# Channel neighbours of a stencil: from GpSimd and VectorE sums to accumulating transfers

## The chip, the cores and the metric

The kernel runs on one core of a Trainium2 chip. The metric is the device time of one execution in microseconds. All arithmetic is in float32 (weights of the gated stage are split into a high and a low part of float32r). The engines are called by their short names: PE (TensorE, matmul), DVE (VectorE), ACT (ScalarE), POOL (GpSimd) and SP (SyncE, which here only issues transfers).

## The reference, cut to what matters

Four residual stages follow each other on x of 2 x 2048 x 512 (batch, time, channel). x1 comes from a masked attention pooling. The second stage is a reaction-diffusion step on each batch's 2048 x 512 plane; it is what the change touches:

```python
    def _L1_cond_ref(y, zX, zY, zR, dx, dy):
        yp_x = jnp.pad(y, ((0, 0), (0, 0), (1, 1)), mode='reflect')
        lap_x = (yp_x[:, :, :-2] - 2.0 * y + yp_x[:, :, 2:]) / (dx * dx)
        yp_y = jnp.pad(y, ((0, 0), (1, 1), (0, 0)), mode='reflect')
        lap_y = (yp_y[:, :-2, :] - 2.0 * y + yp_y[:, 2:, :]) / (dy * dy)
        du_dt = zX[:, :, None] * lap_x + zY[:, :, None] * lap_y + zR[:, :, None] * y * (1.0 - y)
        return du_dt
...
    x = x + _L0_cond_ref(x, L0_cond_W1, L0_cond_b1, L0_cond_v, itok_B_0_2)
    x = x + _L1_cond_ref(x, condB_zX[:, None], condB_zY[:, None], condB_zR[:, None], 1, 1)
    x = x + _L2_cond_ref(x, itok_B_0_6, L2_cond_down_w, L2_cond_down_b, L2_cond_up_w, L2_cond_up_b, L2_cond_ln_g, L2_cond_ln_b)
    x = x + _L3_cond_ref(x, L3_cond_tau_ctx, condB_tauraws, ...)
```

So x2 at channel e is a term in x1 at e, a term in its square, the two neighbours in time times zY, and the two neighbours in channel, e-1 and e+1, times zX; at the edges the one neighbour counts twice. The third stage is an adapter (down, relu, up) with layer norm, the fourth a gated recurrence with several 512 x 512 matmuls.

## The kernel before, in words

Time is cut into 32 tiles of 128 rows (16 per batch), and four tiles make a group: 8 groups, counted (batch, j) in the first part and 0 to 7 in the second. Every engine has its order of work written out by hand, with semaphores between engines.

The **first part** (up to about 190 us) makes x1 and x2 for all 32 tiles. A `tile(b, c)` on PE is the pooling matmuls of tile c (`pooled`, L990 and L991) and the time part of the stencil of the tile eight before it (`time_part`, L1001 and L1003: the diagonal and time neighbours as a matrix of 128 x 128, and the rows across tile edges, which SP brings by the small transfers of `edges`). On DVE a tile is `x1` (L1375) and `mix` (L1389), which adds -zR times the square, made by ACT in `squares` (L661) in the group's slot of sqb, to the time part from PSUM. There are two slots in sqb (j % 2), each of one group.

The channel neighbours: POOL's `channel_part` (L541 to L544) adds x1 shifted by one channel either way into one slot, xr[:, 1], with two slivers for the edges. DVE's `stencil` (L1398) adds zX times this sum to the group's slot of sqb, and raises x2_done. SP then stores the group (`store_x2`, L374) to DRAM, except group 0, which goes straight to xr[:, 0]. The next squares of that slot waits for the store, the next channel_part for the stencil.

Group 0 goes on into the adapter within the first part: PE turns it (`x2_transposes`, L1037), ACT evicts that (`x2_evict`, L676), PE multiplies (`down`, L1047), ACT applies relu (L680), PE multiplies again (`up`, L1063 and L1064). Meanwhile `add_rows` on POOL (L550) adds a bias row from DRAM to xr[:, 0] by an accumulating transfer. DVE's `y_sum` (L1454) adds both and waits for that transfer. `ln_moments` on ACT, `rstd` on POOL, `ln_weigh` (L1461) and `ln_apply` (L1467) on DVE are the layer norm; then `x3_transposes`, `x3_evict` on ACT and `x3_lo` on DVE prepare the second part.

The **second part** is a loop over the 8 groups: `front(g)` (first 12 matmuls against wn1, then wg), soma, temporal and output, all of three matmuls for each product; within group g the adapter of group g+1 runs, whose x2 SP loads from DRAM (`load_group`, L98) into xr[:, (g+1) % 2].

Each engine's queue is in order: a wait holds back all that stands behind it. SP's queue holds the loads, edges and stores in the order of its block. What ties squares to the stores is:

```python
                        if n == 2:
                            act.wait_ge(x2_done, 1)
                        elif n > 2:
                            act.wait_ge(x2_out[j % 2], 16 * ((n - 2 + j % 2) // 2))
                        act.activation(sqb[:, j % 2], xb[:, b, part(j)], ACT.Square).then_inc(sq_act, 1)
```

## Time and profile before

| | us |
|---|---|
| median of 3 runs | 756.19 (756.01 to 758.79) |
| the profiled execution's own time | 756.09 |
| its span, first to last instruction | 754.3 |
| PE busy | 711.4 |
| DVE busy | 554.5 |
| ACT busy | 337.4 |
| POOL busy | 117.5 |

The span leaves out 1.8 us of the execution's own time. All rows below come from this one execution. In them "x8" is a count, busy time is in us and a mean in ns; what stands in square brackets or behind the last bar is the idle time of the engine just before, and what ended it. PEld is PE's weight load, which overlaps its matmuls; PEclk is the clock that PE was granted as a share of the full 2.4 GHz. A line number is that of the kernel before. A DMA share of 1 means that the core's 16 DMA engines were all busy.

### The profile page before, as it was taken

How to read it: one execution, taken by the hardware profiler on the slowest of the kernel's cores; microseconds unless marked ns; L12 is line 12 of the kernel's file. 1: busy time of each engine (PE TensorE's matmuls, PEld its weight loads, DVE VectorE, ACT ScalarE, POOL GpSimd, SP SyncE). 2: the span in 40 equal slices, each digit the busy share in tenths (PEclk: the TensorE clock that was granted, in tenths of full speed). 3: DMA queues.
4: the chain of work that ended last, by engine and by line, in shares of the span. 5: the costliest groups of instructions: out<-in, count | busy, mean ns of one | idle time of the engine just before them, and what ended most of it. 6: DMA issues, size and time to landing. Idle time of an engine off the chain costs nothing.

```text
span 754.3 us, 8249 instructions
## 1 busy us (share of the span) xinstructions
PE 711.4 (94%) x2936; PEld 514.9 (68%) x2936; DVE 554.5 (74%) x787; ACT 337.4 (45%) x706; POOL 117.5 (16%) x195
## 2 busy tenths in 40 slices
PE   4998986977899999999999999999999999999986
PEld 1554443534686877787787868786877788687864
DVE  3686894699798669758875986597668758875954
ACT  2244424323445724563465257344724553464144
POOL 5002032244002100210021021002100210111001
PEclk9999998998999999999999999999999999999999
DMA  7993036312620033011303020330033011301001
GB/s 218 373 343 116 15 103 158 120 58 85 221 45 13 1 111 56 1 56 56 56 0 113 12 45 1 112 52 5 1 111 57 0 56 57 56 1 57 0 1 56
DMA packets 35295, 56.55 MB, mean 75 GB/s; under 512 B 6380, under 2 KB 8428, under 8 KB 35254
## 3 DMA queue, kind: packets, MB, share of 16 engines
q1 hardware_dynamic: 27542, 47.62, 18.2%
q0 software_dynamic: 4224, 8.39, 7.1%
q10 hardware_dynamic: 3488, 0.01, 0.3%
q8 instruction: 23, 0.38, 0.2%
q14 instruction: 18, 0.15, 0.1%
HBM read 40.16 MB, written 15.73 MB: 74 GB/s over the span
## 4 chain that ended last, share of the span: by engine, by line
PE 81%; DVE 9%; issue 3%; ACT 3%; DMA 2%; SPq 1%; POOLq 0%; DVEq 0%; POOL 0%; ACTq 0%
PE bank L1007 19%; PE bank L1009 19%; PE bank L1008 19%; PE bank L1047 4%; PE bank L1064 4%; PE bank L903 3%; PE bank L1111 2%; PE bank L1071 2%; PE bank L1001 2%; PE bank L990 2%; PE bank L1037 2%; DVE sqb L1389 1%; DMA x_scratch<-sqb 1%; DMA sqb<-in_xT 1%; DVE sqb L1398 1%
## 5 line engine op out<-in xcount | busy, mean ns | idle before, releaser
L1007 PE MATMUL bank<-xh,wg_l 128*128 128x512 f32 x256 | 104.1, 407 | 0.1
L1009 PE MATMUL bank<-xh,wg_h 128*128 128x512 f32 x256 | 100.2, 391 | 0.0
L1008 PE MATMUL bank<-xl,wg_h 128*128 128x512 f32 x256 | 99.8, 390 | 0.0
L1504 DVE TENSOR_TENSOR_SCAN tr<-alpha,carry,tr 128x512 f32<-128x512 f32 x48 | 58.9, 1268 | 0.0
L1007 PEld LDWEIGHTS bank<-xh,wg_l 128*128 128x128 f32 x256 | 48.3, 189 | 12.5 <-issue 2.7
L1008 PEld LDWEIGHTS bank<-xl,wg_h 128*128 128x128 f32 x256 | 48.1, 188 | 12.1 <-issue 2.0
L1009 PEld LDWEIGHTS bank<-xh,wg_h 128*128 128x128 f32 x256 | 48.1, 188 | 11.0
L1007 PE MATMUL bank<-th,wt_l 128*128 128x512 f32 x128 | 53.5, 418 | 2.0 <-DVE tl L1516 2.0
L1007 PE MATMUL bank<-xh,ws_l 128*128 128x512 f32 x128 | 53.4, 417 | 0.0
L1007 PE MATMUL bank<-wo_h,pl 128*128 128x512 f32 x128 | 50.6, 395 | 0.8 <-DVE pl L1526 0.8
L1483 DVE TENSOR_TENSOR_SCAN hb<-alpha,carry,bank 128x512 f32<-128x512 f32 x24 | 30.5, 1271 | 28.2 <-PE bank L1009 28.2
L1008 PE MATMUL bank<-tl,wt_h 128*128 128x512 f32 x128 | 50.6, 395 | 0.0
L1009 PE MATMUL bank<-th,wt_h 128*128 128x512 f32 x128 | 50.4, 394 | 0.0
L1009 PE MATMUL bank<-xh,ws_h 128*128 128x512 f32 x128 | 49.9, 390 | 0.0
L1008 PE MATMUL bank<-wo_l,ph 128*128 128x512 f32 x128 | 49.9, 390 | 0.0
L1009 PE MATMUL bank<-wo_h,ph 128*128 128x512 f32 x128 | 49.8, 389 | 0.0
L1008 PE MATMUL bank<-xl,ws_h 128*128 128x512 f32 x128 | 49.8, 389 | 0.0
L541 POOL TENSOR_TENSOR xr<-xb 128x2040 f32<-128x2040 f32 x8 | 28.8, 3600 | 133.1 <-DVE sqb L1398 57.0
L1498 DVE SCALAR_TENSOR_TENSOR tr<-wgb,blend_w,mod 128x512 f32<-128x512 f32 x64 | 45.3, 749 | 3.6 <-ACT mod L714 2.8
L1522 DVE SCALAR_TENSOR_TENSOR wide<-wide,soma 128x512 f32<-128x512 f32 x32 | 22.1, 689 | 31.7 <-ACT wide L744 31.7
L728 ACT ACTIVATE carry<-tr 128x2 f32<-128x2 f32 x32 | 6.5, 203 | 85.2 <-DVE tr L1504 85.2
L744 ACT ACTIVATE wide<-bank,bias_temp 128x512 f32<-128x512 f32 x32 | 22.1, 690 | 46.5 <-PE bank L1009 46.5
(220 smaller groups left out, 1593.3 us busy)
## 6 DMA issues: line engine op xcount, KB each, us to landing
xb<-in_x SPq DMA_DIRECT2D x8, 1024.0 KB, 14.5
xr<-rows_scratch POOLq DMA_DIRECT2D x8, 1024.0 KB, 9.6
x_scratch<-sqb SPq DMA_DIRECT2D x7, 1024.0 KB, 4.4
xr<-x_scratch SPq DMA_DIRECT2D x7, 1024.0 KB, 5.6
result<-xr SPq DMA_DIRECT2D x7, 1024.0 KB, 4.3
xb<-in_xT SPq DMA_DIRECT2D x3, 1024.0 KB, 10.9
xt<-in_xT SPq DMA_DIRECT2D x2, 1024.0 KB, 6.6
sqb<-in_xT SPq DMA_DIRECT2D x2, 1024.0 KB, 10.3
```

Source lines behind the costliest of these rows:

```text
L541: po.tensor_tensor(q[:, :, 1:E - 1], xg[:, :, 0:E - 2], xg[:, :, 2:E], ALU.add)\
L744: act.activation(wide[:, k], bank[TEMP[k]][:], ACT.Tanh, bias=bias_temp[:, k:k + 1], scale=0.5).then_inc(gate_act, 1)
L903: last = pe.matmul(bank[HID[b][j]][:], w1_sb[:, k], xt_slot[b][j][:, k], start=(k == 0), stop=(k == KE - 1))
L1007: pe.matmul(acc, wl, xh_, start=start, stop=False)
L1008: pe.matmul(acc, wh, xl_, start=False, stop=False)
L1009: return pe.matmul(acc, wh, xh_, start=False, stop=stop)
L1047: last = pe.matmul(bank[DOWN][:], dw[:, b, k], x2t(q)[:, k], start=(k == 0), stop=(k == KE - 1))
L1064: pe.matmul(bank[UP(q)[c]][:], z[:, chunk(c)], uw[:, b], start=False, stop=True)\
L1483: ve.tensor_tensor_scan(h, alpha[:, 0:1].broadcast_to([P, GN]), bank[CTX[k]][:], 0.0 if first else carry[:, k, 0:1], ALU.mult, ALU.add)\
L1498: ve.scalar_tensor_tensor(t[:, d], w, blend_w[:, d, k:k + 1], mod[:, d], ALU.mult, ALU.mult).then_inc(tr_in, 1)
L1504: ve.tensor_tensor_scan(t[:, d], alpha[:, 1 + d:2 + d].broadcast_to([P, GN]), t[:, d], 0.0 if first else carry[:, k, 1 + d:2 + d], ALU.mul ...
L1522: ve.scalar_tensor_tensor(wide[:, k], wide[:, k], 1.0, soma[:, k], ALU.add, ALU.mult).then_inc(prod, 1)
```

## The change

The channel neighbours are no longer summed on chip. ACT makes a copy of each group of x1 times zX (`scaled`), 514 wide, with the reflected channel at either edge. It lies where xr[:, 1] was, and 8 elements beyond. SP stores it to a new DRAM tensor (`store_xz`). DVE's mix is now the last step before x2 is stored; the stencil is gone, and with it channel_part. POOL then issues for each group two accumulating transfers (`add_neighbours`): the copy read from its column 0, and, once that has landed, from its column 2, each 512 wide, added in DRAM to x2 (for group 0, in SBUF to xr[:, 0]). load_group waits for these additions.

```diff
+                    def add_neighbours(q):
+
+                        dst = xr[:, 0] if q == 0 else x2_g[:, q:q + 1].rearrange("p u c e -> p (u c) e")
+                        src = xz_g[:, q:q + 1].rearrange("p u c e -> p (u c) e")
+                        po.wait_ge(xz_out, 16 * (q + 1))
+                        if q == 0:
+                            po.wait_ge(mixed, GT)
                         else:
-                            po.wait_ge(x2_done, k)
...
+                            po.wait_ge(x2_out[q % 2], 16 * ((q + 1) // 2))
+                        for i in (0, 2):
+                            if q or i:
+                                po.wait_ge(xz_add, 16 * (2 * q + i // 2))
+                            po.dma_start(dst, src[:, :, i:i + E], accum_op=ALU.add).then_inc(xz_add, 16)
...
-                    for j in range(NG):
-                        channel_part(0, j)
+                    add_neighbours(0)
+                    add_neighbours(1)
                     po.wait_ge(rows_out, 16 * B)
                     add_rows(0)
-                    channel_part(1, 0)
-                    channel_part(1, 1)
                     for c in range(GT):
                         rstd(ln_ss, ss_a, EPSILON, rs_a, c, ln_p, ln_rs, c)
-                    channel_part(1, 2)
-                    channel_part(1, 3)
+                    add_neighbours(2)
...
+                        if g + 3 < GROUPS:
+                            add_neighbours(g + 3)
...
+                    def scaled(b, j):
+                        n, xg, zx_b = NG * b + j, xb[:, b, part(j)], coef[:, ZX, b:b + 1]
+                        act.wait_ge(x1_done, NT * b + GT * (j + 1))
+                        if n:
+                            act.wait_ge(xz_out, 16 * n)
+                        else:
+                            act.wait_ge(masks_set, S_MASKS)
+                        act.activation(xz[:, :, 1:E + 1], xg, ACT.Copy, scale=zx_b).then_inc(xz_set, 1)
+                        act.activation(xz[:, :, 0:1], xg[:, :, 1:2], ACT.Copy, scale=zx_b).then_inc(xz_set, 1)
+                        act.activation(xz[:, :, E + 1:E + 2], xg[:, :, E - 2:E - 1], ACT.Copy, scale=zx_b)\
+                           .then_inc(xz_set, 1)
...
+                    def store_xz(b, j):
+                        u = NG * b + j
+                        sp.wait_ge(xz_set, 3 * (u + 1))
+                        sp.dma_start(xz_g[:, u:u + 1].rearrange("p u c e -> p (u c) e"), xz).then_inc(xz_out, 16)
+
                     def store_x2(b, j):
                         u = NG * b + j
-                        sp.wait_ge(x2_done, u + 1)
+                        sp.wait_ge(mixed, GT * (u + 1))
...
                     edges(0, 3)
+                    store_xz(0, 3)
                     store_x2(0, 1)
...
                     edges(1, 2)
+                    store_xz(1, 2)
                     store_x2(1, 0)
                     edges(1, 3)
+                    store_xz(1, 3)
                     store_x2(1, 1)
```

On SP each store_xz stands right behind its group's edges, ahead of the stores of x2 that stood there. On ACT's queue the squares move behind the scaled copies and edge_high, and from the first evictions on to other places. Three places show it. First, ACT from the squaring of group (0, 2) on to the eviction of the transposed x2 (`prob<-bank`); `probT<-bank` is probT_evict, `edge_hl` edge_high. Before:

```order
L661 ACTIVATE sqb<-xb 128x2048
L636 ACTIVATE g_hl<-bank 128x512
L642 ACTIVATE bw_hl<-bank 64x512 x2
L668 ACTIVATE edge_hl<-edge,coef 64x512
L642 ACTIVATE bw_hl<-bank 64x512 x2
L651 ACTIVATE probT<-bank 128x512 x2
L661 ACTIVATE sqb<-xb 128x2048
L651 ACTIVATE probT<-bank 128x512 x2
L668 ACTIVATE edge_hl<-edge,coef 64x512
L661 ACTIVATE sqb<-xb 128x2048
L676 ACTIVATE prob<-bank 128x512 x4
```

Now, from the same squaring on (`xr_all<-xb,coef` is scaled; xr and xz are now views of xr_all):

```order
L692 ACTIVATE sqb<-xb 128x2048
L670 ACTIVATE probT<-bank 128x512 x4
L680 ACTIVATE xr_all<-xb,coef 128x4x512
L681 ACTIVATE xr_all<-xb,coef 128x4
L682 ACTIVATE xr_all<-xb,coef 128x4
L699 ACTIVATE edge_hl<-edge,coef 64x512
L692 ACTIVATE sqb<-xb 128x2048
L680 ACTIVATE xr_all<-xb,coef 128x4x512
L681 ACTIVATE xr_all<-xb,coef 128x4
L682 ACTIVATE xr_all<-xb,coef 128x4
L707 ACTIVATE prob<-bank 128x512 x4
```

The squaring of (0, 2) stood ahead of the block evictions (`bw_hl`) and stands behind them now, right ahead of the probT evictions; that of (0, 3) stood between these and follows scaled(0,3) now.

Second, ACT at the layer norm of group 0 (`hb,ss_a` are its moments). Before, squares(1,1) and its edge row stand ahead of the first moments:

```order
L661 ACTIVATE sqb<-xb 128x2048
L668 ACTIVATE edge_hl<-edge,coef 64x512
L686 ACTIVATE nmu_a<-sum_a 128x1
L689 ACTIVATE hb,ss_a<-tr,nmu_a 128x512
L686 ACTIVATE nmu_a<-sum_a 128x1
```

Now, from the last moments on:

```order
L717 ACTIVATE nmu_a<-sum_a 128x1
L720 ACTIVATE hb,ss_a<-tr,nmu_a 128x512
L692 ACTIVATE sqb<-xb 128x2048
L680 ACTIVATE xr_all<-xb,coef 128x4x512
L681 ACTIVATE xr_all<-xb,coef 128x4
L682 ACTIVATE xr_all<-xb,coef 128x4
L699 ACTIVATE edge_hl<-edge,coef 64x512
L692 ACTIVATE sqb<-xb 128x2048
```

squares(1,1) follows all four moments now, and scaled(1,2) lies between it and squares(1,2).

Third, POOL around the row add of group 0. Before, with two groups' sums on either side:

```order
L541 TENSOR_TENSOR xr<-xb 128x4x510
L543 TENSOR_SCALAR xr<-xb 128x4
L544 TENSOR_SCALAR xr<-xb 128x4
L550 DMA xr<-rows_scratch 128x4x512
L541 TENSOR_TENSOR xr<-xb 128x4x510
```

Now:

```order
L559 DMA xr_all<-xz_scratch 128x4x512 x2
L559 DMA x_scratch<-xz_scratch 128x4x512 x2
L564 DMA xr_all<-rows_scratch 128x4x512
L570 TENSOR_TENSOR rs_a<-ss_a,consts 128x1
L572 TENSOR_TENSOR rs_a<-rs_a,consts 128x1
```

The row add stood behind sums on POOL itself; it stands behind four accumulating transfers, of which each but the first waits for the one ahead to land.

Elsewhere: on PE, x2_transposes(0), down(0) and up(0) come two, two and one tiles later; on DVE y_sum(0, 0) comes one tile later and ln_weigh and ln_apply are spread among the tiles. weight_hi waits for the last mix instead of the last stencil. At the start, v, b1, ptype, zx, zy, zr and the profile ids are loaded from ACT's queue, ahead of its ten parameters, not from SP's, so that SP goes straight on with the loads of x transposed; tanh and v's copy wait for v and b1 alone, and PE runs twelve warm-up matmuls on a tile of ones:

```diff
+                    pe.wait_ge(ones_set, 1)
+                    for i in range(WARM):
+                        pe.matmul(bank[REP[0]][:, 0:P], ones[:], ones[:], start=True, stop=True)
+                    pe.wait_ge(w1_in, 16)
                     hidden(0, 0)
                     hidden(0, 1)
+                    pe.wait_ge(v_set, 1)
                     scores(0, 0)
```

## Rows read from the trace of the kernel before

**Rows 1.** The page's head: busy time of each engine

```profile
PE 711.4 (94%) x2936; PEld 514.9 (68%) x2936; DVE 554.5 (74%) x787; ACT 337.4 (45%) x706; POOL 117.5 (16%) x195
```

**Rows 2.** Busy time of each engine by stage: PE, PEld, DVE, ACT, POOL, granted clock, DMA

```profile
100.00:151.40 51.40, 42.50 (x129) 22.34 (x127) 34.77 (x50) 15.94 (x26) 13.32 (x10) 0.90 0.45 126
151.40:188.50 37.10, 27.40 (x76) 14.11 (x74) 35.80 (x36) 11.17 (x17) 18.02 (x17) 0.86 0.20 72
...
201.00:754.00 553.00, 544.51 (x2370) 427.39 (x2368) 406.04 (x555) 266.00 (x590) 66.87 (x127) 1.00 0.16 41
```

**Rows 3.** The chain that ended last, 100 to 135 us: start, us, what

```profile
108.25 5.38 DMA x_scratch<-sqb
...
115.53 1.06 ACT probT L651 x2
...
120.39 4.32 DMA x_scratch<-sqb
...
126.61 1.56 ACT prob L676 x3
...
128.31 5.36 PE bank L1047 x8
```

**Rows 4.** Groups on ACT, 0 to 200 us: busy, mean ns, idle before

```profile
L661 ACT ACTIVATE sqb<-xb 128x2048 f32<-128x2048 f32 x8 | 15.3, 1909 | 57.2 <-DMA x_scratch<-sqb 37.6 <-DVE xb L1375 13.6 <-DVE xr L1398 6.0
```

**Rows 5.** Groups on DVE, 100 to 200 us, same columns

```profile
L1398 DVE SCALAR_TENSOR_TENSOR sqb<-xr,coef,sqb 128x2048 f32<-128x2048 f32 x7 | 16.5, 2352 | 0.3
...
L1467 DVE SCALAR_TENSOR_TENSOR xr<-tr,rs_a,xr 128x512 f32<-128x512 f32 x4 | 5.7, 1464 | 0.0
```

**Rows 6.** Instructions by time, start and us: the last block eviction on ACT, then PE

```profile
99.41 0.59 ACT L642 ACTIVATE bw_hl<-bank 64x512 fp32r<-64x512 f32 x1 [1.17 <-PE bank L991]
...
103.88 1.53 PE L990 MATMUL bank<-xb,probT 128*128 128x512 f32 x2 [2.60 <-DVE g_hl L1370]
...
107.76 1.05 PE L990 MATMUL bank<-xb,probT 128*128 128x512 f32 x2
...
109.97 1.03 PE L972 MATMUL bank<-ident,prob 128*128 128x128 f32 x8
```

**Rows 7.** DMA queues of the page: packets, MB, share of 16 engines' span

```profile
q1 hardware_dynamic: 27542, 47.62, 18.2%
q0 software_dynamic: 4224, 8.39, 7.1%
```

**Rows 8.** Stretches with one accumulating transfer, and with one plain store

```profile
128.00:130.00 2.00, 1.69 (x2) 0.84 (x3) 0.00 (x0) 1.24 (x3) 0.00 (x0) 0.50 1.12 182
266.00:268.00 2.00, 2.00 (x10) 1.64 (x9) 0.00 (x0) 0.00 (x0) 0.00 (x0) 1.00 1.03 383
```

**Rows 9.** DMA issues: count, KB, median us from issue to landing

```profile
xr<-rows_scratch POOLq DMA_DIRECT2D x8, 1024.0 KB, 9.6
x_scratch<-sqb SPq DMA_DIRECT2D x7, 1024.0 KB, 4.4
...
xt<-in_wsoma SPq DMA_DIRECT2D x1, 1024.0 KB, 8.1
```

**Rows 10.** Two instants by time, the last y_sum(0) on DVE, then PE

```profile
150.67 0.69 DVE L1454 SCALAR_TENSOR_TENSOR tr<-bank,xr 128x512 f32<-128x512 f32 x1
...
188.28 0.39 PE L1009 MATMUL bank<-xh,wn_h 128*128 128x512 f32 x1
...
196.87 3.51 PE L1111 MATMUL bank<-nar,wn_rep 128*128 128x512 f32 x4 [2.36 <-ACT nar L704]
```

**Rows 11.** The start by time, all engines

```profile
2.34 0.43 SPq L381 DMA_DIRECT2D v_sb<-in_v  x1
...
5.84 3.14 ACTq L581 DMA_DIRECT2D bias_temp<-in_btemp  x1
...
10.65 1.28 ACT L646 ACT_TABLE_LOAD   x1 [10.65 <-issue]
...
18.95 1.02 PE L916 MATMUL bank<-hid,v_rep 128*128 128x512 f32 x2
```

More of the change, by code:

```diff
@@ L799, in _ @@
                     wg_hi(0, wg_h[:, 0:KE], xt0[:])
-                    squares(0, 0)
+                    scaled(0, 0)
                     weights(1, 1)
@@ L803, in _ @@
                     edge_high(0, 0)
+                    squares(0, 0)
                     weights(1, 2)
                     wg_hi(1, wg_h[:, KE:], xr[:, 0])
-                    squares(0, 1)
                     weights(1, 3)
+                    scaled(0, 1)
                     block_exps(1)
@@ L810, in _ @@
                     prob_exps(1)
+                    squares(0, 1)
                     wg_hi(2, wn1_h[:], xt0[:, :, 0:A])
                     sums_raw(1)
-                    squares(0, 2)
+                    scaled(0, 2)
                     sums_hi(1)
@@ L833, in _ @@
                     act.activation(ln_g_row[:], ln_g_row[:], ACT.Copy, scale=SQRT_E).then_inc(rows2_set, 1)
-                    squares(1, 1)
+                    scaled(1, 1)
                     edge_high(1, 1)
```

128 lines of the change are left out of this document (59 added, 69 removed).

## The prediction

> **What bounds the kernel now.** I read first the busy share of each engine, then the stages, then the chain that ended last, then the groups behind its waits. The page shows TensorE (PE) busy 94% of 754.3 us [rows 1]. By stage [rows 2], PE is busy 544.5 of 553.0 us from 201 us on, at full clock: the loop over the eight groups is PE's own work, and the change puts no instruction of PE, DVE or ACT into it. All that can be won or lost lies before 201 us. From 100 to 151.4 us PE is busy 42.5 of 51.4 us, from there to 188.5 only 27.4 of 37.1 us, with DVE busy 35.8. The chain between 100 and 135 us shows what PE waits for [rows 3]: a store of x2 (5.4, then 4.3 us), for which ACT's next squaring waits, and behind it on ACT's queue the evictions (probT at 115.5, the transposed x2 at 126.6) that PE needs for the adapter at 128.3. ACT stood idle 57.2 us ahead of its eight squarings [rows 4]. So two things bound the stretch: DVE's work, and stores with ACT's queue behind them.
>
> **What DVE gets back.** Eight stencils leave DVE, 2.35 us each (seven in the group shown, the eighth writes xr): 18.8 us [rows 5]. POOL's eight neighbour sums leave too. Beside them ln_apply cost 1.46 us on average; a stencil runs at 0.59 us for 512 columns, 0.7 with an instruction's own start, so its four would give back 3 us more [rows 5]. I take 22 us off DVE, nearly all of it between 90 and 189 us. ACT gets eight scaled copies of 128x2048, each 1.91 us as for a squaring [rows 4], with two slivers of about 0.2: 2.25 us each, 18 us in a queue that had 57 us of idle time ahead of squarings. Both are off the end-setting path only as long as nothing else on ACT or in the DMA queues is late; that is what fails, I think.
>
> **What is added to the DMA engines.** Eight stores of the copy at 1.05 MB and sixteen accumulating transfers of 1.05 MB. The nearest row is the rows' accumulating transfer [rows 9]: 9.6 us from issue to landing. Its queue holds eight, 8.39 MB, 7.1% of 754.3 us: 0.071 x 754.3 / 8 = 6.7 us of all 16 engines each, so 2.9 us lie around it. The plain queue costs 0.182 x 754.3 / 47.62 = 2.9 us for a million bytes, 3.0 for a transfer [rows 7]. While one add runs, the engines are busy 1.12 at 182 GB/s; a plain transfer gives 383 GB/s at 1.03 [rows 8]. An add thus fills the engines by itself. Ten of the sixteen are issued inside the loop, where 69 us per group (553 / 8) hide them. Six adds (groups 0 to 2) and add_rows(0) share 90 to 185 us with plain transfers.
>
> **Stage one, to the last y_sum of group 0** (151.4 us now [rows 10]). ACT runs much as now up to its last block eviction, which ends at 100.0 [rows 6]; then squares(0,2) (1.9) stands ahead of the first probT eviction (0.5), so PE's tile(1,0) starts at 102.5, where now it waits for DVE until 103.9. The next tile takes 2.2 us, 107.76 to 109.97, and the one behind the wait 3.9 at the lower clock; after a wait half as long I take 5.2 for both: 107.7. Eight transposes (0.9), the evictions (0.6) and scaled(0,3) (2.25) end at 111.5. SP then issues store_xz(0,3) and, at 112.1, store_x2(0,1). The second of two such transfers lands 7.0 (4.4 + 3.0 less 0.4) to 8.1 us after its issue [rows 9]: 119.7. Here POOL's order matters. Its queue is in order and each add waits for the one ahead: add one of group 1 is issued at 119.7 and lands 9.6 later, the second is issued, and add_rows(0) right behind it on the same queue, so 2.9 + 2 x 6.7 = 16.3 more: the row add lands at 145.6 at the earliest. In that time SP's queue carries about four plain transfers (the rest of x2(0,2), xz(1,0), x2(0,3), xz(1,1), with wtemp behind them): 4 x 3.0 = 12 us, of which 2.9 fit into the gap between the adds. Shared in turn that is 9.1 us more: 154.7. PE's up(0), a tile later in its order, would be done near 140.5 (squares(0,3) can end only at 121.6, behind the 119.7; then some nineteen microseconds of PE's work), and DVE would stand ready near 143.4; so y_sum(0,0) waits for the row add. Two y_sum, a tile, edge_low, two y_sum: 4.7 us. The end of the stage: 150.3 without sharing, 159.4 with it, against 151.4. By row 8, where one add alone fills the engines, I take 159.4: **+8.0**; the other end is **-1.1**.
>
> The Trainium skill ("DMA: Bandwidth & Descriptors", Anatomy of one DMA) fits a transfer issued by GpSimd with 2.0 us and the bytes over 436 GB/s. The 9.6 us row disagrees: by the rule a megabyte would land in 4.4 us, and this stage would end at 148.1.
>
> **Stage two, to the end of the first 12 matmuls of front(0)** (188.7 us now, so 37.3 after stage one [rows 10]). ACT's order: ln_moments(0,3) 1.4 us, squares(1,1) to +3.3 (DVE's mix(1,4) waits 2.3 us for it), scaled(1,2) to +5.6, then SP issues xz(1,2) and x2(1,0) at +6.0. squares(1,2) waits for the latter: landed at +13.0, squared by +14.9, scaled(1,3) to +17.2, xz(1,3) and x2(1,1) land at +24.6, squares(1,3) ends +26.5. Behind it on ACT stands x3_evict(0), on DVE mix(1,12), mix(1,13) and x3_lo(0): four pairs of evictions at 1.15 us, the last subtraction and three matmuls, 6.1 us, so +32.6. The two adds of group 2 run beside it (POOL issues them after the four rstd, at +2.4 and about +14): the first shares with the first pair of stores, 5.2 us, the second with the tail of the next, 0.5. So +38.3, **+1.0** against now; without sharing +32.6, **-4.7**.
>
> **Stage three, to PE's return to full work.** Now the matmuls for mod start at 196.9 and take 3.5 us at the lower clock, 11.7 us after stage two's end [rows 10]. Afterwards mix(1,15) ends 0.7 us after it; two weight_hi, the table load and the gelu (1.8, 1.8, 1.3, 0.7) give 6.3, and the matmuls 1.8 at full clock: 8.1 or so, **-3.6**. The wait for the last stencil goes.
>
> **The start, 0.** SP drops seven small issues (0.43 us for one [rows 11]) and its big loads begin 4 us sooner, but the same seven go ahead of ACT's others. ACT's table load stands behind its last issue at 10.65, then bw_zeros (2.2 us), then tanh(0,0); one of its issues took 3.14 us in the time of SP's loads. Seven at 0.5 put the load at 14.1, tanh(0,0) ends at 18.3 to 18.9, and PE's first score matmul, at 18.95 now, stays where it is. If ACT's issues stall behind loads that start sooner, +3. The warm-up matmuls stand in PE's idle time.
>
> **Sum**: 8.0 + 1.0 - 3.6 + 0 = +5.4 on the profiled execution's own 756.1 us, which equals the median of 756.2: **761.5 us**. By the terms' own bounds (start, landings a microsecond either way) 758.5 to 767.
>
> **Rivals.**
> Rival A, faster: adds and plain transfers overlap on the engines, since an add may wait on memory more than it moves. Then -1.1 - 4.7 - 3.6 = -9.4: 746.7 us. For it: 22 us off DVE, and the busy share is the packets' time, which can hide idle time. Against it: row 8's 1.12. The skill's "Arbitration" paragraph (same page) has each engine serve its queues in turn, packet by packet; no row here shows two of them at work, and by it the forecast's sum would hold.
> Rival B, no change: half the sharing, (5.4 - 9.4) / 2 = -2.0: 754 us.
> Rival C, the adds into x2 in DRAM are dearer than the row's into SBUF, say 9 us of engine time: the two adds of group 1 bring stage one 4.6 more, 766 us. It decides once they take longer than 8 us.
>
> **Chances.** Forecast 0.42, A 0.32, B 0.20, C 0.06. 0.5% (3.8 us) is about what a measurement of this kernel can tell from no change. Faster 0.33, same 0.23, slower 0.44. Range 746.5 to 767: it reaches A's time, as its 0.32 cannot be left out, and C's.
>
> **What would show it.** Right: y_sum(0,0) waits for the row add's landing past 150 us; squares(0,3), (1,2), (1,3) wait for x2 stores that land over 9 us after issue; the six early adds land 10 to 15 us after issue; from then on 69 us per group as now. Wrong: stores landing in 5 to 8 us beside an add; y_sum(0,0) waiting for PE; PE's scores before 17 us or after 21; an add that lands in under 7 us; a loop group longer than now, which would mean the late adds hold back load_group.

## The result, and the profile after

The change makes the kernel slower: 770.07 us (median of four runs, 769.68 to 772.44) against 756.1, a ratio of 1.0205 with a 95% interval from 1.0177 to 1.0232. The forecast was 761.5 us with a range from 746.5 to 767: the sign was right, the size was not, and the time lies outside the range. The kernel before, run again beside the experiments, had medians from 754.2 to 756.0 and single runs from 751.3 to 758.4, so differences of two medians below about 2 us are not read here.

| profiled execution | before | after |
|---|---|---|
| own time / span, us | 756.09 / 754.3 | 769.78 / 768.0 |
| PE's second batch of score matmuls begins | 24.14 | 34.57 |
| end of stage one (last y_sum of group 0) | 151.36 | 165.20 |
| end of stage two (first 12 matmuls of front(0)) | 188.67 | 204.61 |
| end of the first mod matmuls | 200.38 | 211.92 |
| one group of the loop | 70.48 | 71.01 |

The page of the kernel after, the busy times (against [rows 1]), the DMA queues (packets, MB, share of 16 engines' span; against [rows 7]) and the DMA issues (count, KB each, median us to landing; against [rows 9]):

```profile
PE 720.4 (94%) x2960; PEld 521.7 (68%) x2960; DVE 527.8 (69%) x779; ACT 356.4 (46%) x730; POOL 102.0 (13%) x187
...
q1 hardware_dynamic: 30900, 56.04, 21.3%
q0 software_dynamic: 12672, 25.17, 20.1%
q10 hardware_dynamic: 4354, 0.02, 0.4%
...
x_scratch<-xz_scratch POOLq DMA_DIRECT2D x14, 1024.0 KB, 11.0
xz_scratch<-xr_all SPq DMA_DIRECT2D x8, 1028.0 KB, 7.6
...
xr_all<-rows_scratch POOLq DMA_DIRECT2D x8, 1024.0 KB, 9.8
x_scratch<-sqb SPq DMA_DIRECT2D x7, 1024.0 KB, 7.6
```

DVE lost 26.7 us of work and POOL 15.5, and PE is busy for the same share of the span as before. The change did what it says; the time went elsewhere. The same split into stages as in [rows 2], of the kernel after (length, then busy time of PE, PEld, DVE, ACT, POOL, granted clock, DMA share, GB/s):

```profile
110.43:165.20 54.77, 43.06 (x123) 23.55 (x124) 23.64 (x41) 21.66 (x34) 7.12 (x8) 0.89 0.97 249
165.20:204.61 39.41, 27.68 (x71) 14.53 (x70) 20.82 (x33) 18.17 (x25) 3.97 (x6) 0.76 0.65 165
211.92:766.00 554.08, 547.57 (x2373) 426.89 (x2371) 406.82 (x556) 267.46 (x590) 78.50 (x137) 1.00 0.29 63
```

In stage one the DMA engines are now busy 0.97 of the time where it was 0.45. DVE is busy 23.6 us of 54.8 (before: 34.8 of 51.4). Stage two has PE at 27.7 of 39.4 us. The loop (last row) is PE's own work as before, 547.6 of 554.1 us.

The start, instructions by time (start and duration in us; in square brackets the idle time before and what ended it), against [rows 11]:

```profile
8.57 3.57 ACTq L594 DMA_DIRECT2D bias_g<-in_bg  x1
12.18 2.49 ACTq L594 DMA_DIRECT2D bias_soma<-in_bsoma  x1
14.70 2.88 ACTq L594 DMA_DIRECT2D bias_temp<-in_btemp  x1
17.60 3.22 ACTq L594 DMA_DIRECT2D bias_n<-in_bn  x1
20.85 1.28 ACT L665 ACT_TABLE_LOAD   x1 [20.85 <-issue]
...
25.18 2.05 PE L955 MATMUL bank<-hid,v_rep 128*128 128x512 f32 x2 [9.46 <-ACT hid L621]
```

Four issues of ACT take 2.5 to 3.6 us each, the table load stands behind them and comes at 20.85 instead of 10.65 us, and PE waits 9.46 us for the first tanh. PE's second batch of score matmuls begins 10.4 us later than before. Then the waits the forecast spoke of, on POOL, DVE and ACT:

```profile
128.11 1.28 POOL L559 DMA_DIRECT2D x_scratch<-xz_scratch  x1 [15.69 <-DMA x_scratch<-sqb]
141.38 1.25 POOL L559 DMA_DIRECT2D x_scratch<-xz_scratch  x1 [11.99 <-DMA x_scratch<-xz_scratch]
142.13 1.83 POOL L564 DMA_DIRECT2D xr_all<-rows_scratch  x1
...
160.46 0.69 DVE L1488 SCALAR_TENSOR_TENSOR tr<-bank,xr_all 128x512 f32<-128x512 f32 x1 [6.86 <-DMA xr_all<-rows_scratch]
...
127.68 1.91 ACT L692 ACTIVATE sqb<-xb 128x2048 f32<-128x2048 f32 x1 [7.51 <-DMA x_scratch<-sqb]
...
183.87 1.91 ACT L692 ACTIVATE sqb<-xb 128x2048 f32<-128x2048 f32 x1 [12.57 <-DMA x_scratch<-sqb]
...
195.24 1.91 ACT L692 ACTIVATE sqb<-xb 128x2048 f32<-128x2048 f32 x1 [6.57 <-DMA x_scratch<-sqb]
```

The x2 store lands 7.5 us after ACT is ready for squares(0,3). POOL issues the two adds of group 1 at 128.1 and 141.4, and the row add 0.8 us behind the second; it lands 18 us later (DVE goes on at 160.46, having waited 6.86). squares(1,2) waits 12.57 us, squares(1,3) 6.57.

Last, the first matmul of two groups of the loop, in the kernel after:

```profile
272.66 0.39 PE L1046 MATMUL bank<-xh,wn_l 128*128 128x512 f32 x1
...
343.67 0.39 PE L1046 MATMUL bank<-xh,wn_l 128*128 128x512 f32 x1
```

and in the kernel before, the same two groups:

```profile
260.76 0.39 PE L1007 MATMUL bank<-xh,wn_l 128*128 128x512 f32 x1
...
331.24 0.39 PE L1007 MATMUL bank<-xh,wn_l 128*128 128x512 f32 x1
```

71.01 us for a group against 70.48. PE's busy share hides it, since PE is busy nearly all the time in both.

The difference of the spans, 13.7 us, is then: start +10.4, stage one +3.4 (130.6 against 127.2 us from the second score matmuls), stage two +2.1, stage three -4.4, the rest +2.2. The rest is the loop up to its last group, nearly seven groups at +0.53 or 3.6 us, less a last group 1.4 us shorter. The span behind the last group's first matmul is either near 69.2 or near 70.8 us in the traces of all kernels of this study, whatever the change. For that, and for when the first loads land, the experiments are read by their stages first.

### The profile page after: what moved, and what is told of

Read it like the earlier page. It is cut to its first block, busy times and chain, and to the rows that moved or that the text cites. A ratio compares the mean times of both kernels' runs of the same rounds, so it can differ in the third digit from the quotient of the medians.

```text
span 768.0 us, 8320 instructions
## 1 busy us (share of the span) xinstructions
PE 720.4 (94%) x2960; PEld 521.7 (68%) x2960; DVE 527.8 (69%) x779; ACT 356.4 (46%) x730; POOL 102.0 (13%) x187
## 3 DMA queue, kind: packets, MB, share of 16 engines
q10 hardware_dynamic: 4354, 0.02, 0.4%
## 4 chain that ended last, share of the span: by engine, by line
PE 79%; DMA 6%; DVE 6%; issue 3%; ACT 3%; ACTq 3%; POOL 0%; SPq 0%; POOLq 0%; DVEq 0%
PE bank L1048 19%; PE bank L1046 19%; PE bank L1047 19%; DMA x_scratch<-sqb 4%; PE bank L1103 3%; PE bank L1086 3%; PE bank L942 3%; DMA xr_all<-rows_scratch 2%; ACTq L594 2%; PE bank L1150 2%; PE bank L1029 2%; PE bank L1076 2%; PE bank L1110 2%; PE bank L1040 1%; PE bank L955 1%
## 5 line engine op out<-in xcount | busy, mean ns | idle before, releaser
L1047 PEld LDWEIGHTS bank<-xl,wg_h 128*128 128x128 f32 x256 | 48.1, 188 | 13.7 <-issue 1.9
L1040 PE MATMUL bank<-xb,uw 128*128 128x512 f32 x64 | 38.8, 692 | 13.4 <-DVE sqb L1432 13.4
```

The lines of the kernel that those rows point to most:

```text
L1040: pe.matmul(acc, time_m[:, b], xb[:, b, c], start=True, stop=False)
L1047: pe.matmul(acc, wh, xl_, start=False, stop=False)
```

## The experiments

Two theories to begin with. S, for the start: ACT's issues stall. D, for stages one and two: an add fills the DMA engines, so that plain stores and the row add beside it are late. Rivals: R1, the start's delay is absorbed later; R3, ACT's longer queue and the order of the stores. The code cuts of this part are shortened: a line names what moved, not the code word for word. "The kernel with the start undone" is s1_start_back, and a stage one is counted from PE's second score matmuls.

### s1_start_back: the start undone

```diff
 sp: w1; load_xt(0, 0)
+sp: b1, v, ptype, zx, zy, zr, profile
 sp: load_xt(0, 1..3); load_x(0, 0..3)
...
-act: v, b1, ptype, zx, zy, zr, profile
 act: the ten parameter loads
```

> The changed kernel, with the seven small loads (b1, v, ptype, zx, zy, zr, profile) back on SP between load_xt(0, 0) and load_xt(0, 1), as before; the warm-up matmuls and all of the stencil's change stay. Theory S: the seven loads on ACT push ACT's issues into the time of SP's big loads, where one takes 2.5 to 3.6 us, so the table load comes at 20.85 us where it came at 10.65, and all behind it is 10.4 us late. It expects tanh(0,0) back at 14.5 us, PE's first scores at 19 us and 770.1 - 10.4 = 759.7 us. Rival R1, the start's delay is mostly taken up later by waits that are there anyway (the row add, the stores of x2): 764 us or more.

Measured: 764.3 us (763.1 to 767.1). Table load at 11.46, second scores at 26.11 us: 8.5 us of the 10.4 came back there, 5.7 of the medians, 6.7 of the two profiled executions. S's 759.7 is missed by 4.6 us, and the median lies at the edge of what R1 gave (764 or more). But R1's reason, that later waits take the delay up, is not what the trace shows. Of the 3.7 us missing between the profiled executions, 2.0 us is this execution's own start (PE waited 3.7 us for xT's second part), 1.6 us is stage one (132.2 us from the second scores, after: 130.6). Its remainder against the kernel before, without the start's 2.0, is +5.0 in stage one, +2.3 in stage two, -4.4 in stage three and +2.1 behind it.

### s2_start_alone: only the start, in the kernel before

```diff
-sp: seven small loads between load_xt(0, 0) and load_xt(0, 1)
+act: the same seven ahead of the ten parameter loads
+pe: twelve warm-up matmuls ahead of hidden(0, 0)
```

> The kernel before, with the change of the start alone (seven small loads on ACT ahead of its ten, SP's big loads sooner, twelve warm-up matmuls); the stencil as before. Theory S: 756.1 + 10.4 = 766.5 us. Rival R1: 756 to 762 us, since in this kernel too stores and POOL would take up a part.

Measured: 764.1 us (761.9 to 766.2), ratio 1.011 (1.006 to 1.016). The profiled execution has 766.23, 10.1 more than before, with second scores at 34.44 and stage one at 161.1: the delay goes through whole. The median has it at 8.0, between R1's 762 at most and S's 766.5. R1 falls, and S's size is an upper end: the start costs 8 to 10 us in this kernel too, which has the old stencil.

### s3_params_on_sp: the ten parameter loads on SP

```diff
-act: ten parameter loads behind the seven
+sp: the ten, behind load_x(0, 3)
```

> The changed kernel, with ACT's ten parameter loads moved to SP behind the last load_x(0, 3), the seven small ones staying on ACT. It tells the count of issues on ACT from the order of the seven. Theory S (what hurts is ACT issuing at all after SP's big loads began to queue): ACT's seven end at 4.5 us, the table load comes there, tanh(0,0) follows PE's hidden(0,0) at about 11.4 us instead of 24.35, and PE is steady some 2 us sooner than before: 770.1 - 12 = 758 us, 755 to 761. Rival R2 (the first scores wait for the small loads' data, not for ACT's issues, since their packets queue behind SP's): tanh(0,0) not before 18 us, 764 us or more.

Measured: 769.5 us, no gain where I expected 755 to 761. The first half of theory S held: table load at 4.70, first scores at 15.59 instead of 25.18. But the same loads now stall SP. SP's issues and PE's next wait:

```profile
14.82 4.63 SPq L396 DMA_DIRECT2D taus<-in_tau_ctx  x1
...
38.49 0.50 SPq L350 DMA_DIRECT2D xt<-in_xT  x1
...
43.75 4.73 PE L942 MATMUL bank<-xt,w_sb 128*128 128x512 f32 x6 [10.05 <-DMA xt<-in_xT]
```

SP spends 14.8 to 30 us on them, load_xt(1, 0) goes out at 38.49 where it went at 28.16, and PE waits 10.05 us for it. R2 got its time (764 or more) but not its reason, as the first scores came before 18 us. The stall thus belongs to these loads in this stretch, not to ACT.

### s12_x_late: x behind hidden(0, 0)

```diff
 sp: load_xt(0, 0..3)
+sp: wait hid_mm >= 1
 sp: load_x(0, 0..3)
```

> The changed kernel with one wait more: SP issues the four loads of x (4 MB) only when PE has ended hidden(0,0), near 11 us, instead of at 3.9 us. All seventeen small loads stay on ACT in the same order. Theory S1 (ACT's issues stall since SP's large loads are queued in the DMA engines in that time, not since there are seventeen of them): ACT's last issue ends near 10 us instead of 20.8, tanh(0,0) comes at 14 to 15 us, PE's scores at 16 to 19, the whole 9 to 11 us less than the change: 759 to 761 us. Rival S2 (small loads on ACT's queue get slow behind one another after the first ten, whatever SP does): the last issue still ends after 17 us and the time stays over 766 us.

Measured: 770.1 us, no change:

```profile
11.41 3.31 SPq L354 DMA_DIRECT2D xb<-in_x  x4
...
20.65 1.28 ACT L666 ACT_TABLE_LOAD   x1 [20.65 <-issue]
```

The loads of x go 7.5 us later, ACT's table load still comes at 20.65. Theory S1 as I had put it, that the loads of x are the cause, falls. Rival S2 got its numbers, and it was the next run that told it from the right one. In 12 to 21 us the trace of the kernel after has these two queues (q1 is SP's, q10 ACT's small loads; packets, MB, share):

```profile
q1 hardware_dynamic: 1605, 3.19, 98.2%
q10 hardware_dynamic: 1604, 0.01, 11.7%
```

1605 packets of about 2 KB and 1604 of a few bytes: one for one. In the kernel before, in 6 to 12 us, SP's queue had little behind its seven small issues and moved 0.77 MB. In those 6 us the two queues show:

```profile
q1 hardware_dynamic: 1254, 0.77, 40.6%
q10 hardware_dynamic: 2471, 0.01, 22.9%
```

2471 small packets in 6 us, 412 a microsecond, against 178 a microsecond above. With x late, SP's queue had moved 2.7 MB by 12 us, less than the 4 MB of xT, so xT alone kept it filled until x followed. The Trainium skill ("DMA: Bandwidth & Descriptors", Queues, rings and completion order, its paragraph on arbitration) has each DMA engine go round the queues packet by packet; 1605 to 1604 agrees, in packets as the profile counts them.

### s14_gap: SP's queue kept dry until ACT's loads have landed

```diff
 sp: load_xt(0, 0)
+sp: wait params_in (all ten)
 sp: load_xt(0, 1..3); load_x(0, 0..3)
```

> The changed kernel, in which SP issues load_xt(0, 1) and all large loads behind it only when ACT's ten parameter loads have landed; the seventeen small loads stay on ACT in the same order. Between 12 and 21 us the changed kernel's traces show 1605 packets of SP's queue (2 KB each) and 1604 of ACT's (4 bytes mostly): one for one. In the kernel before, SP's queue ran nearly dry from 6 to 12 us, and ACT's moved 2471 packets in that time. Theory P (ACT's loads are thousands of packets of a few bytes, which queue packet for packet behind SP's large ones, and an issue waits for room in the queue): with SP's queue dry behind load_xt(0, 0), ACT's last issue ends near 11 us, all its packets are through by 13 us, and PE's scores, now behind load_xt(0, 1), begin near 20 us, so that PE is steady near 26 us instead of 34.6: 760 to 763 us. Rival S2 (ACT's issues stall by their own number): last issue after 17 us, 768 us or more.

Measured: 763.7 us (761.9 to 764.4), 6.4 less than the change, with all seventeen loads on ACT in the same order. ACT's last issue and table load, and the two queues in 6 to 12 us:

```profile
9.84 0.53 ACTq L596 DMA_DIRECT2D bias_n<-in_bn  x1
10.39 1.28 ACT L667 ACT_TABLE_LOAD   x1 [10.39 <-issue]
```

```profile
q10 hardware_dynamic: 4063, 0.02, 36.7%
q1 hardware_dynamic: 128, 0.23, 9.9%
```

No issue takes over 1.3 us, the last ends at 10.4, and 4063 small packets pass in 6 us, 677 a microsecond. Second scores at 27.52 (expected 26), and the time 0.7 us above P's 760 to 763. S2 falls: the number of issues on ACT was the same. What theory P says of the two queues holds; that a stalled issue waits for room in its queue is inferred, since a trace shows how long an issue takes and not what it waits for. The change closed the gap in SP's queue in which these 4354 packets used to get through (3488 of them on ACT before).

### s4_no_adds: the start undone, no adds

```diff
 add_neighbours(q):
-    two dma_start(dst, src, accum_op=add)
-pe, sp: waits on xz_add
+pe: wait mixed >= GT;  sp: wait x2_out[1] >= 16
```

> As the kernel with the start undone, and without the sixteen accumulating transfers of the neighbours: nothing is issued, and what waited for them waits for mix or for the stores of x2. The neighbours in channel are left out of x2. The scaled copies and their stores stay. Theory D (an add keeps all DMA engines busy for 6.4 us, so plain stores and the row add beside it are longer): the row add lands within 10.5 us of its issue and y_sum(0,0) waits for PE or DVE at about 143, stage one ends at 148, stores of x2(1,0) and x2(1,1) land in 7 us each; 12 to 13 us less than with the start undone: 747 us, 744 to 750. Rival R3 (ACT's longer queue, the scaled copies and the stores' waits without any sharing, is what offsets DVE's 22 us): within 4 us of the kernel with the start undone, 756 us or more.

Measured: 751.5 us (749.9 to 753.5), 12.8 less than with the adds. D's 12 to 13 less held; its 744 to 750 was counted from the 759.7 expected of the start undone, and is missed by 1.5. The form is the one that theory D gave: stage one 125.5 us from the second scores instead of 132.2, stage two 34.7 instead of 39.6, y_sum(0,0) without a wait. R3 falls. But half of what R3 names is still there. ACT's waits for stores of x2, with no add beside them:

```profile
120.23 1.91 ACT L688 ACTIVATE sqb<-xb 128x2048 f32<-128x2048 f32 x1 [7.69 <-DMA x_scratch<-sqb]
...
163.54 1.91 ACT L688 ACTIVATE sqb<-xb 128x2048 f32<-128x2048 f32 x1 [6.61 <-DMA x_scratch<-sqb]
...
174.88 1.91 ACT L688 ACTIVATE sqb<-xb 128x2048 f32<-128x2048 f32 x1 [6.54 <-DMA x_scratch<-sqb]
```

squares(0,3) waits 7.69 us as it did with the adds; squares(1,2) waits 6.61 instead of 12.3. So even without adds, and with 26.7 us of DVE's work gone, stage one is only 1.7 us shorter than in the kernel before (125.5 against 127.2) and stage two 2.6 us. And a group of the loop takes 71.01 us here too, so the loop's 0.53 us has nothing to do with the late adds.

### s9_plain_copies: copies instead of adds

```diff
-po.dma_start(dst, src[:, :, i:i + E], accum_op=ALU.add)
+po.dma_start(dst, src[:, :, i:i + E])
```

> The kernel with the start undone, in which the sixteen transfers of the neighbours are plain copies and not accumulating ones (same source, target, size, queue and waits; x2 becomes one shifted copy, which leaves out the rest of the second stage). The adds were 6.4 to 6.7 us of all engines each and 11.0 us from issue to landing. Theory M (it is the accumulation, not the transfer from DRAM to DRAM or the queue of POOL, that fills the engines): a copy takes 3 us of the engines and lands 5 to 6 us after its issue, and most of the 12.8 us between this kernel with and without adds is gained: 753 to 756 us. Rival M2 (a transfer from DRAM to DRAM costs as much without the addition): 762 us or more.

Measured: 752.7 us, 11.6 of the 12.8 us between the kernels with and without adds. POOL's queue and the transfers' landing (with the adds, in the kernel with the start undone: 20.0% of 761.2 us, and 11.4 us):

```profile
q0 software_dynamic: 8576, 25.17, 14.8%
...
x_scratch<-xz_scratch POOLq DMA_DIRECT2D x14, 1024.0 KB, 6.7
```

The eight row adds of the same queue cost 6.9% of 750.5 us in the kernel without the others, 51.8 us. That leaves 59.4 us for sixteen copies, 3.7 each, and (152.2 - 51.8) / 16 = 6.3 us for an add. M's numbers for a copy were low (3 us of the engines and 5 to 6 us to landing expected, 3.7 and 6.7 measured), but M holds in kind and M2 falls: of an add's 6.3 us, a copy the same way costs 3.7.

### s5_rows_first: the row add ahead of group 1's adds

```diff
 add_neighbours(0)
-add_neighbours(1)
 add_rows(0)
+add_neighbours(1)
```

> The kernel with the start undone, in which POOL issues the row add of group 0 (add_rows(0)) ahead of the two adds of group 1 instead of behind them. With the start undone alone, the row add was issued at 135.0 us, landed 18.4 us later, and y_sum(0,0) began at 153.5, some 6.5 us after DVE stood ready for it; the kernel's median was 764.3 us. Theory D (the row add is late since it shares the engines with group 1's second add and plain stores): now it is issued when PE has turned x2, near 129 to 131, lands in 10 to 13 us, y_sum(0,0) no longer waits for it, and begins at about 147: 5 to 6 us less, 757 to 760 us. Group 1's adds go later, to 130 to 165 us, where group 2's first store can meet them: if that costs, up to 3 us come back. Rival R4, the wait at y_sum is not what sets the end: 762 us or more.

Measured: 752.3 us (750.8 to 754.4), 12 less where I expected 5 to 7. POOL's issues, and y_sum(0,0):

```profile
127.31 1.28 POOL L571 DMA_DIRECT2D xr_all<-rows_scratch  x1 [22.77 <-PE bank L1077]
128.06 1.85 POOL L566 DMA_DIRECT2D x_scratch<-xz_scratch  x1
...
144.08 0.68 DVE L1489 SCALAR_TENSOR_TENSOR tr<-bank,xr_all 128x512 f32<-128x512 f32 x1
```

The row add is issued at 127.3, y_sum(0,0) waits for nothing, and stage one takes 122.4 us from the second scores, 9.8 less; stage two 36.7, 2.9 less. The wait was 6.5 us of that. Another 1.7 stood already at squares(0,3), ahead of anything that this run changes, and is scatter of the executions; some 1.6 us came between there and y_sum, where group 1's adds no longer run beside the stores. The last part is inferred, no run takes it by itself. R4 falls.

### s8_x2_first: stores of x2 ahead of the copies' stores

```diff
 edges(0, 3)
-store_xz(0, 3)
 store_x2(0, 1)
+store_xz(0, 3)
...
-store_xz(1, 2)
 store_x2(1, 0)
+store_xz(1, 2)
...
-store_xz(1, 3)
 store_x2(1, 1)
+store_xz(1, 3)
```

> The kernel with the start undone, in which SP issues store_x2 ahead of store_xz at the three places where both stand together (x2(0,1) ahead of xz(0,3), x2(1,0) ahead of xz(1,2), x2(1,1) ahead of xz(1,3)). With the start undone alone, squares(0,3), (1,2) and (1,3) waited 7.6, 12.3 and 6.8 us for those stores, each issued behind the scaled copy and its store. Theory Q (the order in the queue is half of what these waits cost: a store of x2 stands behind a scaled copy of 2.3 us and a store of 1.05 MB, 3 us of the engines): the three squares come 4 to 5 us earlier each; the last two waits are a chain that sets stage two's end, and the sum is 6 to 10 us: 755 to 758 us. Rival D2 (the adds' share of the engines alone makes the stores late, not the order): 761 us or more.

Measured: 749.5 us (747.7 to 751.3), 14.8 less where I expected 6 to 10; with the start undone and this alone it is faster than the kernel before, ratio 0.9925 (0.990 to 0.995). ACT's squares:

```profile
115.44 1.91 ACT L693 ACTIVATE sqb<-xb 128x2048 f32<-128x2048 f32 x1 [3.93 <-DMA x_scratch<-sqb]
...
162.09 1.91 ACT L693 ACTIVATE sqb<-xb 128x2048 f32<-128x2048 f32 x1 [1.04 <-DMA x_scratch<-sqb]
...
174.69 1.89 ACT L693 ACTIVATE sqb<-xb 128x2048 f32<-128x2048 f32 x1
```

The waits of 7.6, 12.3 and 6.8 us are 3.9, 1.0 and none. Stage two takes 28.0 us instead of 39.6. A scaled copy stood ahead of each store in two queues: the store waited for ACT's copy, and shared the engines with the copy's store. No run tells these two apart. Theory Q holds, and gives more than its 6 to 10 us; D2 falls: with the adds still there, the swap takes 11.6 us out of stage two, where taking the adds away took 4.9.

### s6_before_spread: the kernel before with a mended start

```diff
 (the change's start, in the kernel before)
-act: seven of the parameter loads ahead of the table load
+act: four of them behind tanh(0, 2), three behind tanh(0, 3)
```

> The kernel before with the changed start (seven small loads on ACT, SP's big loads sooner, warm-up matmuls), and eight of ACT's ten parameter loads mended: the first three stay where they are, four are issued behind tanh(0,2) and three behind tanh(0,3), when SP's first loads have landed. The stencil as before. With ten on SP the scores began at 15.6 us (before: 18.95) but SP's own next loads came 10 us late. Theory S: ACT's ten issues end near 6 us, PE's scores begin at 15.6 us, nothing is late behind, and the kernel is 3.3 us faster than before: 752 to 753.5 us against 756.1. Rival R5 (issues on ACT stall until 20 us wherever they stand, or the parameters come too late for block_exps): 756 us or more.

Seven loads moved in fact, four and three, where the expectation says eight. Measured: 757.4 us (753.2 to 760.3), no gain where I expected 3.3 us. The scores began at 15.03, 3.9 us sooner, and at the end of stage one nothing of it was left (151.35 against 151.36). PE waited 2.2 us for load_xt(1, 0) and 1.9 for ACT, which waited 6.6 us for the last parameter load. R5's time came (756 or more), by its second reason. In this kernel, what the start gains, the next loads take.

### s11_rows_x2: both orders changed

```diff
 (s5_rows_first and s8_x2_first together)
```

> The kernel with the start undone and both changes of order together: add_rows(0) ahead of group 1's adds on POOL, store_x2 ahead of store_xz on SP at the three places. Alone they measured 752.3 and 749.5 us, against 764.3. With store_x2 first alone, y_sum(0,0) still waited 8.7 us for the row add, and stage one ended at 154.9 us, stage two 27.7 us later. Theory D+Q (both wait chains are independent: the row add sets stage one, the stores set stage two): stage one ends at 147, stage two takes 28 to 31, the sum is 741 to 745 us, 11 to 15 less than before. Rival D3 (group 1's adds, pushed from 116 to 140 us into 128 to 155 us, make the stores of stage two late, as the gain of one is paid with the other): 747 to 752 us.

Measured: 739.3 us (737.0 to 744.1), ratio 0.980 (0.977 to 0.982). Stage one takes 119.3 us from the second scores, stage two 34.0; squares(1,2) and (1,3) wait again, 5.9 and 3.9 us, as group 1's adds are there now. So D3 is right in kind for this execution (stage two gives back 6 us of 11.6), while the median is 1.7 us under the 741 to 745 of D+Q.

What stage two gives back is not the same in every execution. These are POOL's second transfer of that stage and squares(1,3), first here and then in s18_pad128 (below), which has the same two orders:

```profile
155.06 1.28 POOL L566 DMA_DIRECT2D x_scratch<-xz_scratch  x1 [6.33 <-DMA x_scratch<-xz_scratch]
167.73 1.91 ACT L693 ACTIVATE sqb<-xb 128x2048 f32<-128x2048 f32 x1 [3.87 <-DMA x_scratch<-sqb]
```

```profile
159.99 1.28 POOL L567 DMA_DIRECT2D x_scratch<-xz_scratch  x1 [9.92 <-DMA xz_scratch<-xr_all]
163.67 1.90 ACT L694 ACTIVATE sqb<-xb 128x2048 f32<-128x2048 f32 x1
```

Here the add goes out at 155.06, ahead of the store of x2(1,1) at 157.51, and squares(1,3) waits 3.9 us for that store. There it goes out at 159.99, behind the store at 158.05, squares(1,3) doesn't wait, and stage two takes 27.9 us. The other traces with both orders have the add first and 33.7 to 35.3 us. The profiled execution of this kernel is also its slowest of six, 744.1. That the six runs' range of 7 us comes from these two outcomes fits, but is not shown.

### s13_rows_x2_late: the same with the change's own start

```diff
 (s11_rows_x2, with the start of the change, and s12_x_late)
```

> The changed kernel, its start kept, with all three: the loads of x behind hidden(0,0), the row add ahead of group 1's adds, x2's stores ahead of the copies'. Theory S1 and D+Q: as the kernel with the start undone and both orders changed, within 3 us, 740 to 746 us, since the small loads' place is then worth nothing either way. Rival S2: 750 us or more.

Measured: 752.0 us (746.8 to 754.0). Table load at 18.98, second scores at 32.80, 8.7 us later than in s11_rows_x2. S2's 750 or more is met. The expectation of "within 3 us" rested on the delay of x mending the start, and that s12_x_late had disproved. The difference, 12.6 us of the medians and 6.5 of the profiled executions, is the start's price once more, with the scatter of s11_rows_x2 in it.

### The loop: s17_before_shift and s15_pad

The first is the kernel before with 32 unused bytes of each partition behind xr, the second the kernel after with 32 more behind xr_all (64 in all).

```diff
 xr = sb("xr", [P, 2, GT, E])
+sb("shift", [P, 8])
```

> The kernel before, with nothing changed but 8 unused elements (32 bytes of each partition) declared behind xr. Theory L: a group of the loop takes 71.01 us instead of 70.48 and the kernel 756.1 + 4.2 = 760.3 us. Rival L2: 70.48 us and no change.

> The changed kernel, with 8 unused elements (32 bytes of each partition) declared behind xr_all, so that every tile behind it lies 64 bytes, not 32, further on than in the kernel before. In every kernel with the new stencil a group of the loop takes 71.01 us, also in the one without adds; in the kernel before and in the one with the start changed alone 70.48. The matmuls of wn and wg, 108 of a group, follow each other at 233.3 ns there and at 229.0 ns before. Theory L (it is the 32 bytes by which xr_all is longer than xr: tiles that PE reads lie at another offset): 70.48 us for a group again, 8 x 0.53 = 4.2 us less: 766 us. Rival L2 (the later adds and load_group, or the order of DVE and ACT around them, cost PE half a microsecond for each group): 71.01 us as now and 769 to 771 us.

Measured for the first: 758.5 us (755.7 to 761.7), ratio 1.0054 (1.003 to 1.0079), and for a group of the loop

```profile
261.10 0.39 PE L1008 MATMUL bank<-xh,wn_l 128*128 128x512 f32 x1
...
332.11 0.39 PE L1008 MATMUL bank<-xh,wn_l 128*128 128x512 f32 x1
```

71.01 us: the kernel before takes on the longer group by nothing but the shift. L2 falls. Its median is 3.5 us above that of the kernel before run beside it (754.96), and seven groups at +0.53 give 3.7. Measured for the second: 768.2 us, a group at 70.90 us, where I had expected 70.48 and 766 us. The place of the tiles decides, but 64 bytes don't restore it.

The traces also narrow down which matmuls are slower. Those of xh and xl against wg follow each other at 229.0 ns (median) in the kernel before and at 233.3 in the kernel after and in s17_before_shift. Those of ws, wt and wo stay at 227 in all three. By the order of declaration wg lies ahead of xr and is not moved, while xh and xl lie behind it and are; ws, wt and wo and what they are multiplied with lie all behind it and move together. So it is not the place of xh alone, as ws is multiplied with xh too. That the distance of the two operands decides fits, but no run tests it.

### The best version: s16_rows_x2_pad, s18_pad128, s19_pad512

s11_rows_x2 with 8, 24 and 120 unused elements behind xr_all: 64, 128 and 512 bytes in all.

> The kernel with the start undone and both orders changed (739.3 us), with the 8 unused elements behind xr_all. Theory L: 735 us, 733 to 738, about 20 less than before. Rival L2: 739 to 740 us.

> The kernel with the start undone and both orders changed, with 24 unused elements behind xr_all, so that the tiles behind it lie 128 bytes further on than in the kernel before. A group of the loop took 70.48 us with the tiles of before, 71.01 with 32 bytes more (in the changed kernel and in the one before alike), 70.90 with 64. Theory L128 (tiles that PE reads want the same offset within 128 bytes): 70.48 us for a group and 4 us less than without it, 735 to 736 us. Rival L0 (no simple rule of the offset): 70.6 to 71.0 us and 738 to 741 us.

> As the one with 24 unused elements, but 120, so that the tiles lie 512 bytes further on than before. Theory L128, and a rule by 512 bytes too: 70.48 us for a group, 735 to 736 us. If 128 bytes more gave 71 and this gives 70.48, the period is 512. Rival L0: 70.6 to 71.0 us.

Measured: 741.5, 742.4 and 737.3 us. A group takes 70.90 us in the first, 70.92 to 70.98 in the second and, with 512 bytes,

```profile
246.58 0.39 PE L1048 MATMUL bank<-xh,wn_l 128*128 128x512 f32 x1
...
317.06 0.39 PE L1048 MATMUL bank<-xh,wn_l 128*128 128x512 f32 x1
```

70.48 us again. The first two missed the 735 to 736 us expected, and L128 falls with s18_pad128. Ratio of s19_pad512 to the kernel before 0.9736 (0.968 to 0.979): the lowest median here, with an interval that overlaps that of s11_rows_x2 (0.977 to 0.982). The gain is seen in the groups, 7 x 0.53 = 3.7 us; the medians (739.3 and 737.3, ranges of 7 us each) show a part of it at most. Between 128 and 512 bytes nothing was tried, so whether the rule is 512 stays open.

## Why the prediction was wrong

**The start, 0.** This is the step that failed, +10.4 us. It was priced as seven issues of 0.5 us ahead of ACT's others, with +3 if they stall. I had the row that warned: one issue at 3.14 us [rows 11]. I read it as a single stall in the time of SP's loads and did not ask what it waited for. The seven issues taken off SP were a pause in SP's queue, and ACT's small packets passed in that pause. By s14_gap the stall goes when the pause is put back. By s3_params_on_sp and s12_x_late it stays when the loads move to SP or x comes later. A sum of issue times could not hold it: the same issues took 0.4 to 1.3 us in s14_gap and up to 3.6 in the kernel after. With the start undone the kernel measured 764.3 us, 2.8 above the forecast, but this nearness is partly luck: stage one was 3.0 too dear, the loop and the start 2 us each too cheap. The sign did not hang on the start: that kernel is slower than the one before too (ratio 1.013, 1.009 to 1.018).

**Stage one, +8.0.** Measured +3.4 in the kernel after and +5.0 with the start undone. The mechanism was right in each part: y_sum(0,0) waited for the row add, issued 0.8 us behind group 1's second add, past 150 us; the first of those adds landed 13 us after its issue. The sum was off in two terms. scaled(0,3) was done 2.4 us sooner than the 111.5 of the forecast (119.5 less the start's 10.4), and the sharing cost 6.9 us instead of 9.1: from the landing of x2(0,1) at 127.6 to that of the row add at 160.4 there are 32.8 us, where the forecast had 25.9 without sharing and 35.0 with. The kernel without adds ends the stage 6.7 us sooner, but there the row add has no add ahead of it either, and y_sum(0,0) waits for nothing: that is the price of order and sharing together, as far as DVE is ready to use it.

**Stage two, +1.0.** Measured +2.1: 39.4 us where the forecast had 38.3. The first pair of stores, with an add beside it, landed 12.7 us after issue, the next 6.7. Without adds it was 34.7 (forecast 32.6). That squares waits behind two queues for its store, which s8_x2_first shows, was in the forecast's working as a given; I costed the order instead of asking what a swap of two issues would save.

**Stage three, -3.6.** Measured -4.4, 7.3 us instead of 8.1.

**The loop, as now.** The second error. The change puts no instruction of PE, DVE or ACT into the loop, and I looked no further. It made a tile 32 bytes longer, which moved the tiles behind it, and a group took 71.01 us instead of 70.48: 3.6 us up to the last group, of which the span shows 2.2, the last group's end being 1.4 shorter. (The forecast's 69 us per group was 553 / 8; between two like matmuls it is 70.48 in the kernel before.) In the forecast's list of what would prove it wrong, a longer group was meant to be load_group held back by the late adds; s4_no_adds and s17_before_shift exclude that.

**The rivals.** A (no sharing, 746.7 us) fell: s4_no_adds shows what the adds cost beside the stores. B had half the sharing, but measured was three quarters (6.9 of 9.1) in stage one and, by the kernel without adds, five sixths (4.9 of 5.7) in stage two. C (dearer adds in DRAM) fell: 6.3 to 6.4 us each, no more than the row add's 6.7 worked out from [rows 7]. With the start at 0 and the loop as before, the measured terms give +1.1 (3.4 + 2.1 - 4.4), where the forecast had +5.4. The start's +10.4 lies also outside the +3 that the forecast gave to stalled issues.

## What to carry to other kernels

Before small loads are moved to another queue, count their packets, not only their issues, and look at what the other queues hold in that time: here thousands of packets of a few bytes needed a stretch with little other traffic. Where an engine waits next for one transfer, issue it ahead of those that are waited for later; two such changes of order turned 764 us into 739. And after a change of a tile's size, compare the period of a loop that the change does not touch, between two like instructions, since busy shares do not show it.

## What the runs showed of the hardware

- Small packets (ACT's loads of 4-byte elements) passed at 178 a microsecond beside a full queue of 2 KB packets, one for one with them (1604 to 1605 in 9 us), at 412 where that queue took 40.6% of the engines' time and at 677 where it took 9.9%. Issues of small loads took up to 3.6 us (on ACT, kernel after) and 4.6 us (on SP, s3_params_on_sp) beside a full queue, and 1.3 at most on ACT in s14_gap.
- A transfer of 1 MB from DRAM to DRAM took 3.7 us of all sixteen engines and 6.7 us from issue to landing as a copy, 6.3 to 6.4 and 11.0 to 11.4 as an addition (medians of fourteen, with other traffic beside them).
- With the tiles behind a 16 KB tile at 0, 32, 64, 128 and 512 bytes from where they were, a group of the loop took 70.48, 71.01, 70.90, 70.92 to 70.98 and 70.48 us, and the 32 bytes did the same in two kernels. Only the matmuls of wg with xh and xl changed their pace (229.0 and 233.3 ns), those of ws, wt and wo kept 227. Why, no run shows.
